# A second pair of index buffers in the scatter pass of a graph network kernel

## The reference

```python
edge_index = jnp.stack([src, dst])
x = _layernorm(x + _L0_gnn_ref(x, edge_index, W1, b1, W2, b2))          # edge MLP, segment_max over dst
x = _layernorm(x + _L1_gnn_ref(x, edge_index, edge_attr_64, u, ...))    # mean of edge_attr over src, MLP
x = _layernorm(x + _L2_gnn_ref(x, src, dst, W_gc, b_gc, W_lin, b_lin))  # mean of x[src] over dst
x = _layernorm(x + _L3_gnn_ref(x, ntype, etype, src, dst, ...))         # typed attention over dst
```

```python
sums = jax.ops.segment_sum(edge_attr, src, num_segments=n_nodes)
cnt = jax.ops.segment_sum(jnp.ones((edge_attr.shape[0],)), src, num_segments=n_nodes)
```

## Time and profile before

| | us |
|---|---|
| median of 3 runs | 19607.6 |
| lowest and highest | 19588.42, 19612.66 |
| the profiled execution's own time | 19425.3 |
| its span in the profile | 19423.5 |

### The profile page before, as it was taken

How to read it: one execution, slowest core, us unless ns; L and a number is a source line. 1 busy time by engine, 2 the same in 40 slices (tenths; PEclk the granted TensorE clock), 3 DMA queues, 4 the chain that set the end, 5 groups by cost and what they waited for, 6 DMA issues and landing times.

```text
span 19423.5 us, 125968 instructions
## 1 busy us (share of the span) xinstructions
PE 4712.7 (24%) x20806; PEld 3710.9 (19%) x20806; DVE 7110.8 (37%) x16320; ACT 1013.1 (5%) x4397; POOL 13120.1 (68%) x13050
## 2 busy tenths in 40 slices
PE   3221221221666666666510000000032000000002
PEld 2100010000566665566410000000021000000001
DVE  5444444443333433333331111111123444444444
ACT  0000000000000000000000000000022000000000
POOL 4666666667666666666657777777755666666665
PEclk9655555555555555555555555555566555555555
DMA  2222222221333333333211121211123333333332
GB/s 71 76 70 68 69 69 67 66 70 51 93 93 91 91 92 93 92 93 93 71 41 45 47 47 47 47 47 47 45 84 121 97 97 97 95 95 97 97 95 55
DMA packets 1464730, 1467.46 MB, mean 76 GB/s; under 512 B 727134, under 2 KB 1226293, under 8 KB 1464536
## 3 DMA queue, kind: packets, MB, share of 16 engines
q1 hardware_dynamic: 1029704, 830.45, 14.2%
q0 software_dynamic: 416960, 533.81, 12.1%
q10 hardware_dynamic: 18000, 102.41, 1.3%
HBM read 863.04 MB, written 602.69 MB: 75 GB/s over the span
## 4 chain that ended last, share of the span: by engine, by line
issue 31%; another core or an unknown queue 19%; DVE 18%; POOL 17%; PE 10%; DVEq 2%; DMA 2%; ACT 1%; SPq 0%; POOLq 0%; ACTq 0%
POOL gat L643 16%; PE pair L1011 4%; DVE oh_lo L1294 2%; DVE prod L1306 2%; DVE oh_hi L1296 2%; PE bank L1000 2%; DVE cur L1391 1%; DVE run_sb L1661 1%; DMA gat<-tab_t,gi 1%; DVE ar L1684 1%; DVE ag_idx L1310 1%; PE bank L1002 1%; PE bank L988 1%; DVE run_sb L1693 1%
## 5 line engine op out<-in xcount | busy, mean ns | idle before, releaser
L600 POOL DMA_INDIRECT perm<-at,ag_idx x3125 | 3135.3, 1003 | 1575.6 <-issue 937.5
L643 POOL DMA_INDIRECT gat<-tab_b,gi x3125 | 3121.2, 999 | 1588.0 <-issue 968.1
L643 POOL DMA_INDIRECT gat<-tab_x,gi x3125 | 3307.4, 1058 | 1191.1 <-issue 1187.7
L643 POOL DMA_INDIRECT gat<-tab_t,gi x3125 | 3027.8, 969 | 1373.5 <-issue 902.5
L1032 PE MATMUL pair<-ident,tails 128*64 128x128 f32 (+1 forms) x20 | 4.9, 421 | 8795.8 <-DVE tails L1474 4423.6
L1011 PE MATMUL pair<-blk,ohb 128*128 128x65 f32 x7500 | 1765.3, 422 | 12.5 <-DVE ohb L1416 12.3
L1032 PEld LDWEIGHTS pair<-ident,tails 128*64 128x64 f32 (+1 forms) x20 | 3.1, 170 | 8797.5 <-DVE tails L1474 4424.4
L1584 DVE TENSOR_TENSOR run_sb<-p,gat 128x320 f32<-128x320 f32 x625 | 314.9, 504 | 3702.2 <-DMA gat<-tab_x,gi 3691.9
L1011 PEld LDWEIGHTS pair<-blk,ohb 128*128 128x128 f32 x7500 | 1645.8, 329 | 88.0 <-DVE ohb L1416 14.0
L961 PE MATMUL bank<-oh_s,lo_bf 128*128 128x490 bf16 x625 | 368.2, 589 | 3219.1 <-DVE prod L1306 2638.4
L1290 DVE TENSOR_TENSOR oh_s<-iota_bf,st_sh 128x490 bf16<-128x490 bf16 x625 | 417.6, 668 | 1760.3 <-remote 1431.9
(11 more groups left out here) (283 smaller groups left out, 9830.6 us busy)
## 6 DMA issues: line engine op xcount, KB each, us to landing
edge<-start_rows SPq DMA_DIRECT2D x250, 800.0 KB
run<-run_sb SPq DMA_DIRECT2D x250, 800.0 KB
blk<-perm SPq DMA_DIRECT2D x750, 165.0 KB
run<-run_sb SPq DMA_DIRECT2D x125, 900.0 KB
at<-in_edge_attr SPq DMA_DIRECT2D x625, 160.0 KB
start_rows<-zeros ACTq DMA_DIRECT2D x125, 800.0 KB
tab_t<-trow SPq DMA_DIRECT2D x98, 512.0 KB
perm<-at,ag_idx POOLq DMA_INDIRECT x3125
```

The source lines that it names most:

```text
L600: pool.indirect_dma_start(perm_d, rows(perm_d, ag_idx[tp][:, k, s:s + 1]), at[tp][:, s, k, :], None).then_inc(a_sc[tp], 16)
L643: pool.indirect_dma_start(gat[:, k, s, 0:width], None, table, rows(table, gi[tp][:, s, k:k + 1])).then_inc(g_in[k], 16)
```

## The change

A second pair of index buffers `sc_idx` is added, and the scatters read their ranks from it. ACT copies `ag_idx[tp]` to `sc_idx[tp]` once all five rank columns of the tile are written and tile t-2's scatters have landed, and counts `a_cp` up: by 5 in the first tile, where it copies column by column, by 1 in each later tile. So tile t's copy is `a_cp` = t + 5. DVE no longer waits for landings; before tile t it waits for `a_cp` = t + 3, the copy of tile t-2. POOL waits for the whole tile's copy before its first transfer instead of for each rank column (the first tile keeps its waits by column). ACT stages parts two tiles ahead, after the ranks of tile t rather than t-1, and writes the key column in tile t for tile t itself, just before the copy.

```diff
@@ SyncE, before the passes over the edges
-            sp.wait_ge(a_col, T + 1)
+            sp.wait_ge(a_col, T)
@@ GpSimd
             def scatter(t, tp, first):
                 pool.wait_ge(a_ld[tp], t * (8 * SUB) + (16 * SUB if tp == 0 else 8 * SUB))
                 pool.wait_ge(a_col, t + 1)
+                if not first:
+                    pool.wait_ge(a_cp, t + KS)
                 pool.nop(nofuse=True)
                 for k in range(KS):
-                    pool.wait_ge(a_idx, t * KS + (k + 1))
-                    pool.nop(nofuse=True)
+                    if first:
+                        pool.wait_ge(a_cp, k + 1)
+                        pool.nop(nofuse=True)
                     for s in range(SUB):
                         pool.indirect_dma_start(
-                            perm_d, rows(perm_d, ag_idx[tp][:, k, s:s + 1]), at[tp][:, s, k, :], None
+                            perm_d, rows(perm_d, sc_idx[tp][:, k, s:s + 1]), at[tp][:, s, k, :], None
                             ).then_inc(a_sc[tp], 16)
@@ ScalarE
             key_column(0, 0)
+            stage_a(1, 1)
@@ ScalarE, phase_a
-                if not first:
-                    act.wait_ge(a_idx, t * KS)
-                stage_a(t + 1, 1 - tp)
-                if not first:
-                    scattered(act, t + 1, 1 - tp)
-                key_column(t + 1, 1 - tp)
+                if first:
+                    for k in range(KS):
+                        act.wait_ge(a_idx, k + 1)
+                        act.activation(sc_idx[tp][:, k, :], ag_idx[tp][:, k, :], ACT.Copy).then_inc(a_cp, 1)
+                    stage_a(t + 2, tp)
+                    return
+                act.wait_ge(a_idx, t * KS + KS)
+                if not isinstance(t, int) or t < T - 1:
+                    stage_a(t + 2, tp)
+                if not isinstance(t, int) or t >= 2:
+                    scattered(act, t, tp)
+                key_column(t, tp)
+                act.activation(sc_idx[tp][:], ag_idx[tp][:], ACT.Copy).then_inc(a_cp, 1)
@@ VectorE, phase_a
                 if not isinstance(t, int) or t >= 2:
-                    scattered(v, t, tp)
+                    v.wait_ge(a_cp, t + (KS - 2))
```

4 lines of the change are left out of this document (3 added, 1 removed).

## The result

The changed kernel takes 19780.97 us, the median of 4 runs (19767.32 to 19790.94), against 19606.25 us (19588.42 to 19612.66) of the kernel before: a ratio of 1.009, 95% interval 1.0073 to 1.0108. It is 175 us slower, where 72 us less were forecast, and 51 us above the upper end of the range. Its profiled execution took 19767.32 us, the span 19765.5 us.

What follows compares the result with a forecast made beforehand. The scatter pass was taken as bound by GpSimd's transfers (4070 us) plus 515 us of waiting for ranks. Main part -22 and first tiles -50 gave -72 us: 19535.6 us timed, own range 19475 to 19570, whole range 19340 to 19730 us.

Steps and rivals of the forecast that it cites:

- What bounds the kernel: Scatter pass: 4070 us at GpSimd's own pace plus 515 us waiting for ranks, slowed by TensorE steps up to 19.6 us.
- VectorE's wait: Before each tile, its wait for scatters of two tiles back is removed: between 0 and -44 us.
- 7.5 quick steps: Main part: after each GpSimd pause 7.5 quick rank steps, then 2.0 slow; one 7.1 us pause per two tiles, -22 us.
- rival A: Whole-tile wait costs more than the lead wins: +130 to +180 us, about 19740 us; chance 0.27.
- The price of a pause: GpSimd at a tile's edge: 7.1 us for one missing step with the copy, 3.25 us for each further one.
- `zeros` transfer: On ScalarE, may come earlier by a tile; size kept, GpSimd's pace beside it unchanged, taken at nothing.
- First tiles: Tiles 1 to 14: with ScalarE's wait one tile older, pauses fall to the later rate, -50 us; bounds 0 and -103.
- GpSimd's lost waits and SyncE: GpSimd loses four of five rank waits a tile, SyncE's loads still wait for tile t-2: both worth nothing.
- The transfers: Scatter transfers beside VectorE's work: the share of slower ones may grow by 16 us at most; 0 taken.
- The 182 us between profile and timed runs: Profiled execution of the kernel before was 182 us under the timed median; difference carried over as it is.
- theory N: From the experiments: TensorE's answers come one by one, 2.8 us apart, whichever matmul; a slow step is 7 answers.
- B: Experiments' rival to theory N: each signal between engines is late, three in a step, whatever the matmuls.

Runs made afterwards that it cites:

- no_lead: Changed kernel, but VectorE also waits, as before, for the transfers of the tile before the last; 1.0085, 19613.34 us.
- coarse_only: Kernel before, but after the first tile GpSimd waits for a tile's last rank column before its first transfer; no copies; 1.0049, 19545.84 us.
- order_back: Changed kernel with ScalarE's key column back ahead of the products, for the next tile, and the copy right behind the last ranks; 1.0025.
- fine_copy: Changed kernel, but ScalarE copies and GpSimd waits by the single rank column in every tile; 1.0019, 19479.68 us.
- before_again: Kernel before, unchanged, run and profiled again; 0.9997, 19436.79 us.
- fine_no_lead: Changed kernel with copies and waits by the column, and VectorE waiting for the transfers of the tile before the last; 0.9997.
- group 1: First follow-up runs, four kernels on one chip, changing one part at a time; the kernel before took 19437.07 us there.
- after_again: Changed kernel, unchanged, run on a chip without late answers; 1.0034, 17100.6 us.
- before_h1: Kernel before with one histogram matmul for each column instead of five, on a chip without late answers; 1.0001.
- after: The changed kernel in its first measurement and profile; 1.009, 19780.97 us.
- no_lead_b: Changed kernel with VectorE also waiting for the transfers of the tile before the last, on a chip without late answers; 1.0000, 16994.51 us.

## Why the prediction was wrong

**What bounds the kernel: right.** The pass, its 4070 us of transfers and 515 us of waiting, slow steps of up to 19.6 us, and their end shortly after GpSimd stops, are all in the profile after as they were in the earlier trace rows.

**VectorE's wait: right at its end of zero.** It was priced at 0 to 44 us. The wait is gone from the list, and `no_lead` (1.0085) against the changed kernel (1.009) finds no gain. "It shortens the pass only if the earlier steps fall in a quick stretch" was the right condition; the trace of `no_lead` adds that they can't, since an idle VectorE gets its quick steps afterwards.

**The step that failed: 7.5 quick steps.** From there came 9.5 of 10 columns, one missing and 7.1 us a pause. The profile shows 6,'s lower value, and two missing columns in all but one of the 54 pauses. That was rival A's condition, "6 quick steps rather than 7.5", and its mechanism. Taking the middle between 6 and 10 was the mistake: those counts came from two pauses, which ended at different columns. After the change all pauses end alike, with a tile just complete, and 41 of the 53 cycles between them begin with six quick columns, the others with five. As no step may be half there, 9.5 of 10 was no state of the kernel at all. The count of pauses (55) was right, their length wrong: 390 us were forecast, 636.6 came, and 547.8 in `no_lead`, which has two missing columns in 54 of its 55 pauses, on a chip where the kernel before waits 421.0 us.

**The price of a pause: mis-sized.** Two missing columns were to cost 7.1 + 3.25 = 10.4 us; `coarse_only` shows 9.5 us, `no_lead` 9.96 us, the changed kernel 11.8 us. Of the copy's 0.6 us, the stagings that were put ahead of it in the queue make it 1.6 us from the last rank to the next transfer, against 0.8 us before. Those stagings were in the change's own lines and were left out of the sum. (Of the `zeros` transfer, taken at nothing, the prediction says that the earlier trace rows show GpSimd's pace beside it; they don't.) Whether the other 1.8 us between `no_lead` and the changed kernel are the lead (in the cycles shown its eighth column is there 8.8 us before GpSimd stops, that of `no_lead` 10.6 us) or the chip stays open, because no chip with late answers came again.

**First tiles: wrong sign.** The start of the pass was in no term: the first ranks, ready at 127 us, now wait on ScalarE until 141 us, +14 us. Behind it, -50 us, with bounds of 0 and -103, was forecast; +66 us came. The step "with that wait one tile older I expect the later rate" freed ScalarE's products from the landing of the tile before, but they went from there into TensorE's late answers (`bst` after 19.6 us of "remote"), and a whole-tile wait then exposes five steps at once, 26 us. `coarse_only`, with the old order, has 114.8 us there instead of 165.4, so the part of ScalarE's changes in it is measured. That it is the products' early start in particular was only argued, as `order_back` ran on no chip where it could show, and `fine_copy` speaks against the early start alone: its products are freed in the same way, and it waits 74.9 us there, 18 us less than `before_again`. Only together with the whole-tile wait does it cost anything. The bounds should have had an upper side: a wait that goes lets work begin, and where it begins something else may be slow.

**GpSimd's lost waits and SyncE: right.** They were put at nothing; the issue time before the transfers is 933.6 us, 937.5 us before, and no wait for loads beyond 0.3 us stands before them.

**The transfers: the bound had the wrong side for these chips.** 0 to +16 us was kept; they got 61 us shorter (984 ns), and 14 and 56 us shorter in `coarse_only` and `no_lead`. On the chips without late answers they got 48 us longer. The argument from VectorE's share of overlapping work gave neither size; what counts there is where in a tile its row of one-hots begins; on the chips with late answers the share was not taken apart. The Trainium skill's rule (SBUF — State Buffer, § Who interferes with whom), that a VectorE instruction with two SBUF inputs contends with a GpSimd instruction that reads SBUF, fits the 1.21 and 1.59 us beside those one-hots, and that ScalarE contends with nobody fits `fine_no_lead` at 0.9997. The same section adds, as inferred, that a `tensor_tensor`, which is what `oh_s` is, does not hold up GpSimd's writing of descriptors; the 1.21 and 1.59 us don't agree with that. And the rule gives no size: the same instructions cost 51 us over the pass or nothing more, by their moment.

**The sum.** Forecast -22 - 50 = -72 us. Measured in the profile +224 + 66 + 14 us of waits - 65 us of transfers and issue = +239 us in the pass, more than the 175 us between the timed runs. On one and the same chip `no_lead`, equal in ratio within the interval, has +127 + 73 + 14 - 72 = +141 us in the pass (main part, first tiles, start, transfers and issue) and +176 us in time, of which +91 and +109 us come with the whole-tile wait alone.

**The range.** It left out the worst third of A. The prediction's own figures for A don't quite meet: its 5.2 us a tile against 3.75 are +1.45 us and not +1.2, so the low end of A was 160 us rather than 130. Measured are 636.6/110 = 5.8 us a tile. A's own sum was 19740 us, 41 us below the result, because the first tiles were "unchanged or halved" in it. The 182 us between profile and timed runs, carried over as it was, is now seen in part: the kernel before had a median of 19437 us on the chip of group 1 and 16993 to 17041 us on five others, so two executions can differ by the chip alone, and the first profile's 19425.3 us lie 12 us from the first of these medians. Which chips the first profile and its timed runs had isn't known.

## What to carry to other kernels

Before several fine waits are joined into one, count whole steps: how many the producer has made when the consumer arrives, at the lowest pace seen and not at a middle value. Here the joined wait made every cycle nearly the same, at six quick steps. A longer lead helps only if the producer is as fast while the consumer works as while it pauses; the earlier trace rows said that it isn't. And a copy that lies between producer and consumer is better made by the column (1.0019, against 1.0085 with the copy of a whole tile), with all that only prepares later tiles behind it in its engine's queue; what the order alone is worth where answers are late wasn't measured.

## What the runs showed of the hardware

- Late answers came with the chip. The kernel before waited 113 times for ranks on one chip and took 19437 us; on five others it took 16993 to 17041 us, and the changed kernel on such a chip had one pause of 8.9 us. The gathers behind the pass differ too: in `after_again` GpSimd stands 952.3 us before those of `tab_b`, in `before_again` 1586.2 us.
- Where answers are late, an idle TensorE recovers as well as one whose GpSimd has stopped: two quick steps after 18.1 us of idling in `no_lead`, with transfers going on. The matmuls left out in `before_h1` could not tell theory N from B on the chips to be had.
- The traces of the late chips speak for N all the same. They keep the time at which each signal (semaphore update) of TensorE came, though no view prints it; `oh_s` at 2037.03 us in the profile after starts 0.03 us behind such a signal. A step has three of them, and in the slow steps for which all are in the trace (17 to 22 us from one histogram's signal to the next) they lie as follows, by the lines of the changed kernel: from the histogram's to that of L974, one matmul, 2.79 us in the median of 34 steps of `fine_copy` and 2.61 us in 26 of `after`; from there to L966, one matmul, 2.80 and 2.81 us; from there to L970, five matmuls of which only the last carries a signal, 14.00 and 12.95 us. So it is about 2.8 us for each matmul, signal or not, as N says; by B the three gaps would be alike. Whether each matmul ends late or only its completion is told late, the trace doesn't show.
- TensorE isn't the only thing that is disturbed on such a chip. Of its signals in the main part of `no_lead` 1181 of 1663 are in the trace, in the same kernel on the other chip (`no_lead_b`) all 1590. And SyncE's instruction `MOVE` for the loads, 29 ns in the median of both, takes 2 to 1402 ns in the one and 29 to 39 ns in the other (`no_lead`, then `no_lead_b`: least, median, most; first and last start):

```profile
L439 SPq MOVE at<-in_edge_attr x610: 2/29/1402, 177.5 to 4784.7; - x153
```
```profile
L439 SPq MOVE at<-in_edge_attr x610: 29/29/39, 177.7 to 4095.8; - x153
```

- So a rival that no run tests stands beside "TensorE answers late": that on these chips something common to the engines, the recording of their events among it, holds them up. The cause stays open.
- The granted clock hardly matters to this kernel. Where answers are late, two runs of the kernel before in group 1 had a mean granted clock of 0.757, most others 0.51 to 0.52; they took 19438.04 and 19436.10 us, the median is 19437.07. Where they aren't, with one histogram matmul in a step instead of five the page of `before_h1` shows the full level, 2.4 GHz, through the scatter pass and the gathers of `b`, where `after_again` beside it has the lower one, 1.2 GHz, from the second slice on; the time is within 0.03% of the kernel before on five chips. There the clock and the number of matmuls changed together, and neither shows in the time.

```profile
PEclk9999999999999999999855555555575555555555
```
```profile
PEclk7555555555555555555555555555576555555555
```
